# Moving the slot bookkeeping of an expert router forward, and reordering three VectorE steps of the expert loop

## The chip, the cores and the metric

The kernel runs on one core of a Trainium2 chip. The metric is the device time of one execution in microseconds (us), the median of three runs.

## What is computed

The input is 4096 tokens (16 sequences of 256) with 128 features, in float32. Four layers follow one another, each on the layer norm of `x` and added back to `x`: a gated linear attention, a mixture of experts, a small state-space layer, and a feed-forward layer on FP4-quantised values. The change lies in the mixture of experts alone:

```
scores = x_aD @ router_DE                         # 8 experts, the best one is taken
gates  = sigmoid(score of the best, else -inf)
mid    = silu((gate*x) @ w1[e]) * ((gate*x) @ w3[e])      # 128 -> 352
routed = mid @ w2[e]                              # 352 -> 128
shared = (silu(x @ ws1) * (x @ ws3)) @ ws2        # for every token
x      = x + shared + routed
```

## The kernel before, in words

Every engine has its own instruction stream, and the order in each is written out by hand; semaphores tie them together. There are three blocks with a barrier of all engines between them. `phase_ab` holds attention, and after it the shared expert and the routing. `phase_c` is the loop over the routed experts. `phase_d` does the last two layers.

**The tail of phase_ab.** The shared expert runs in eight groups of 512 tokens. On TensorE, `group(n)` is three `up(n, f)` (six 128x512 matmuls each) with two halves of `down(n-1)` between them. ScalarE applies Silu (`gated_up`), VectorE multiplies the two halves (`hidden`) and adds results to `x` (`add`). `up(n, f)` waits for the `hidden` of two steps before, `down(n, 0)` for the third `hidden` of its group. In the gaps stands the routing. VectorE's `one_hot` finds each token's expert; TensorE's `count_and_rank` counts; VectorE's `bases`, `positions` and `slot_parts` turn that into a slot number for each token; `slot_places` (four parts, L925) and `slot_rows` (L920) write one-hot factors; GpSimd multiplies two copies of the latter by gate and token number (L498, L501); TensorE's `slots` (64 matmuls, L1211) turn them into a table of which token stands in which slot; VectorE's `slot_table` copies the table out (L938); and GpSimd issues indirect DMAs (`gather`, L193, two for each pair of slot tiles, four pairs in this block) that fetch the token rows. In the same gaps ScalarE and GpSimd split the expert weights into high and low parts: `expert_high` (L657) and `expert_low` (L487, which waits for its `expert_high`). The last two gathers of the block stand behind the last `expert_low` on GpSimd.

**phase_c.** 5120 slots are 20 pairs of 128-row tiles. Iteration j of each engine is skewed. TensorE in iteration j: transposes of pair j+1 (L1494), the down product of pair j-2 (L1502), the first up product of pair j, transposes of the hidden values of pair j-1 (L1524), the second up product of pair j (L201 to L203). The transposes of pair k wait for semaphore `s_rg` to reach k+1. It is counted up by VectorE's scaling of the gathered rows of pair k by their gates (L1443), which stands in VectorE's iteration k-2, that is in iteration j-1 as seen from TensorE's iteration j. ScalarE does Silu (L1399) and copies of transposed values (L1406, L1415, L1416). VectorE in iteration j: low part of the transposed rows of pair j+1 (L1429), output copy of pair j-2 (L1436), row scaling of pair j+2 (L1443), hidden products of pair j (L1451, one for each tile), and in iterations 1 to 3 three steps each of FP4 preparation of the last layer's weights (`prepare`). GpSimd gathers pair k once the rows of pair k-4 have been scaled.

Of the kernel before, what the change touches and what calls it, by code (L numbers as in the profile page):

```python
# [205 lines left out]
def phase_ab(nc, io, g):  # L206
# [4 lines left out]
    with ExitStack() as ctx:  # L211
# [197 lines left out]
        def _(pool):  # L409
# [78 lines left out]
                                        w13p[:, 0, :, e, :].bitcast(F32), ALU.subtract).then_inc(s_wl, 1)  # L488

            by_slot = [P, T, SLOTS]  # L490
            for e_ in range(2):
                expert_low(e_)
            pool.wait_ge(s_gate, 1)
            nc.gpsimd.tensor_scalar(gate, gate, 0.5, 0.5, ALU.mult, ALU.add).then_inc(s_one, 1)
            expert_low(2)
            pool.wait_ge(s_pos, 5)
            pool.wait_ge(s_one, 4)
            nc.gpsimd.tensor_tensor(slot_high[:, :, SLOTS:], slot_high[:, :, 0:SLOTS],  # L498
                                    gate.unsqueeze(2).to_broadcast(by_slot), ALU.mult).then_inc(s_one, 1)
            pool.wait_ge(s_one, 5)  # L500
            nc.gpsimd.tensor_tensor(slot_high[:, :, 0:SLOTS], slot_high[:, :, 0:SLOTS],  # L501
                                    small[:, SLOTS + EXPERTS + P:].unsqueeze(2).to_broadcast(by_slot), ALU.mult).then_inc(s_part, 1)
            for e_ in range(3, 5):
                expert_low(e_)
            pool.wait_ge(s_tab, 2)
            for par in range(2):
                pool.wait_ge(s_xn2s[par], 8 * B)
            for k in range(2):
                gather(nc, g, k)
            for e_ in range(5, EXPERTS):  # L510
                expert_low(e_)
            for k in range(2, 4):
                gather(nc, g, k)
# [2 lines left out]
        def _(act):  # L516
# [161 lines left out]
            for n in range(2, GROUPS):  # L678
                for f in range(3):
                    gated_up(n, f)  # L680
                    if f == 0 and n + 1 < GROUPS:
                        token_high(n + 1)
                if n == 2:
                    act.wait_ge(s_hot, 1)
                    nc.scalar.activation(gate, best, ACT.Tanh, scale=0.5).then_inc(s_gate, 1)
                for e_ in ((0, 1), (2,), (3, 4), (), (5, 6), (7,))[n - 2]:
                    expert_high(e_)

        @blk_.vector
        def _(dve):  # L690
# [204 lines left out]
                nc.vector.tensor_tensor_scan(before.rearrange("p e t -> p (e t)"), padded[:, 0:ET],  # L895
                                             restart.rearrange("p e t -> p (e t)"), 0.0, ALU.add, ALU.mult).then_inc(s_hot, 1)

            def bases():
                dve.wait_ge(s_r, 1)
                step(nc.vector.tensor_scalar(over, ps_n, float(P - 1), None, ALU.add))  # L900
                step(nc.vector.tensor_scalar(count, over, 7, 7, ALU.arith_shift_right, ALU.logical_shift_left))
                step(nc.vector.tensor_tensor_scan(upto, ones[:, 0:EXPERTS], count, 0.0, ALU.mult, ALU.add))
                step(nc.vector.tensor_tensor(base, upto, count, ALU.subtract))

            def positions():
                step(nc.vector.tensor_tensor(rank, ps_r, base.unsqueeze(2).to_broadcast(spread), ALU.add))
                step(nc.vector.tensor_tensor(rank, rank, hot, ALU.mult))
                step(nc.vector.tensor_reduce(posf, rank.rearrange("p e t -> p t e"), AX.X, ALU.add))

            def slot_parts():  # L910
                nc.vector.tensor_copy(g["pos"][:, :], posf)
                step(nc.vector.tensor_copy(posi, posf))
                step(nc.vector.tensor_scalar(hii, posi, 7, 7, ALU.arith_shift_right, ALU.logical_shift_left))
                step(nc.vector.tensor_copy(hif, hii))
                step(nc.vector.tensor_tensor(low_pos, posf, hii, ALU.subtract))
# [44 lines left out]
            for n in range(2, GROUPS):  # L960
                for f in range(3):
                    hidden(n, f)
                    if f == 0 and n + 1 < GROUPS:
                        token_low(n + 1)
                    if (n, f) == (2, 2):
                        bases()
                    if (n, f) == (3, 0):
                        positions()
                    if (n, f) == (3, 1):
                        slot_parts()  # L970
                    if (3, 1) <= (n, f) <= (4, 1):
                        slot_places(3 * n + f - 10)
                    if (n, f) == (4, 2):
                        slot_rows()
                    if (n, f) == (6, 1):
                        slot_table()
                    if (n, f) == (6, 2):
                        slot_experts()
                add(n - 1)
            add(GROUPS - 1)  # L980

# [1 line left out]
        def _(pe):  # L983
# [207 lines left out]
            def group(n):  # L1191
                for f in range(3):
                    up(n, f)
                    if f < 2:
                        down(n - 1, f)
# [10 lines left out]
            def slots(part):  # L1206
                if part == 0:
                    pe.wait_ge(s_part, 1)
                pe.wait_ge(s_pos, part + 1)
                for t in range(8 * part, 8 * part + 8):  # L1210
                    last = nc.tensor.matmul(ps_s, slot_low[:, t, :], slot_high[:, t, :], start=(t == 0), stop=(t == T - 1))  # L1211
                if part == 3:
                    last.then_inc(s_tab, 1)
# [25 lines left out]
            up(2, 2)  # L1239
            group(3)  # L1240
            group(4)
            group(5)
            for part in range(4):
                slots(part)
            group(6)
            group(7)
            down(7, 0)
# [51 lines left out]
def phase_c(nc, io, g):  # L1299
# [3 lines left out]
    with ExitStack() as ctx:  # L1303
# [32 lines left out]
        def live(j):  # L1336
            return 0 <= j.off < PAIRS
# [85 lines left out]
        def _(dve):  # L1423
            def body(j):
                if live(j + 1):
                    k = j + 1
                    done(dve, s_xT, k)
                    done(dve, s_u, k, n=2, per=2, ago=2)
                    nc.vector.tensor_tensor(xT[:, k.par, 1, :, :], ps_t[:, 0:2, :], xT[:, k.par, 0, :, :].bitcast(F32),  # L1429
                                            ALU.subtract).then_inc(s_xL, 1)  # L1430
                if live(j + -2):
                    f = j + -2
                    done(dve, s_y, f)
                    if f.off >= 2:
                        dve.wait_ge(s_out[f.par], f.half(16))
                    nc.vector.tensor_copy(y[:, f.par, :, :], ps_y[:, 0:2, :]).then_inc(s_ys, 1)  # L1436
                if live(j + 2):
                    k = j + 2
                    dve.wait_ge(g["s_rows"][k.off % 4], 32 * (k.off // 4 + 1))
                    done(dve, s_xp, k, ago=2)  # L1440
                    for t in range(2):
                        c0 = 2 * k.off + t
                        last = nc.vector.tensor_scalar(rows[:, k.par, t, :], g["rows"][:, k.off % 4, t, :],  # L1443
                                                       g["slot_gate"][:, c0:c0 + 1], None, ALU.mult)
                    last.then_inc(s_rg, 1)
                if live(j):
                    for t in range(2):
                        done(dve, s_act, j, n=t + 1, per=2)
                        if t == 0:
                            done(dve, s_hp, j, n=2, per=2, ago=2)  # L1450
                        nc.vector.tensor_tensor(hid[:, j.par, t, :], act1[:, t, :], ps_3[:, t, 0:F], ALU.mult).then_inc(s_h, 1)  # L1451
                if 1 <= j.off < LO:
                    for n in range(3 * j.off - 3, 3 * j.off):
                        prepare(n)
# [527 lines left out]
```

## Time and profile before

| what | value |
|---|---|
| median of 3 runs | 643.13 us (643.05 to 643.78) |
| the profiled execution: its time / its span | 643.13 us / 641.4 us |
| TensorE matmul busy | 552.9 us (86%) |
| VectorE busy | 456.4 us (71%) |
| ScalarE busy | 306.6 us (48%) |
| GpSimd busy | 346.1 us (54%) |

The span is what the profiler saw between the first and the last instruction; the execution's own time is 1.7 us more. Times of rows count from the span's start. A shift of one block moves all that follows it, since the blocks are separated by barriers. PE is TensorE, DVE VectorE, ACT ScalarE, POOL GpSimd.

### The profile page before, as it was taken

How to read it: one execution, taken by the hardware profiler on the slowest of the kernel's cores; microseconds unless marked ns; L12 is line 12 of the kernel's file. 1: busy time of each engine (PE TensorE's matmuls, PEld its weight loads, DVE VectorE, ACT ScalarE, POOL GpSimd, SP SyncE). 2: the span in 40 equal slices, each digit the busy share in tenths (PEclk: the TensorE clock that was granted, in tenths of full speed). 3: DMA queues.
4: the chain of work that ended last, by engine and by line, in shares of the span. 5: the costliest groups of instructions: out<-in, count | busy, mean ns of one | idle time of the engine just before them, and what ended most of it. 6: DMA issues, size and time to landing. Idle time of an engine off the chain costs nothing. (4 is left out here: it accounts for less than half of the span.)

```text
span 641.4 us, 15224 instructions
## 1 busy us (share of the span) xinstructions
PE 552.9 (86%) x4532; PEld 450.0 (70%) x4533; DVE 456.4 (71%) x1215; ACT 306.6 (48%) x862; POOL 346.1 (54%) x519
## 2 busy tenths in 40 slices
PE   2799999999999997994879999287999999999965
PEld 1457667777776686874779998265787788788754
DVE  2679998999985569542874443127899999899873
ACT  1356667656675542230434444125455555645522
POOL 4468777777775302546654310555666657654221
PEclk9999999999999998997989999688999999999987
DMA  7001001001011432003222210110111110110000
GB/s 204 16 18 43 26 28 50 25 30 44 25 42 59 122 99 67 1 18 85 74 51 57 58 41 26 33 17 9 26 18 16 21 29 16 20 29 10 9 17 16
DMA packets 35320, 25.60 MB, mean 40 GB/s; under 512 B 4752, under 2 KB 31696, under 8 KB 35280
## 3 DMA queue, kind: packets, MB, share of 16 engines
q1 hardware_dynamic: 29392, 20.39, 10.7%
q0 software_dynamic: 5888, 4.72, 4.7%
q8 instruction: 20, 0.33, 0.2%
q14 instruction: 20, 0.16, 0.1%
HBM read 14.09 MB, written 6.82 MB: 33 GB/s over the span
## 5 line engine op out<-in xcount | busy, mean ns | idle before, releaser
L1107 PE MATMUL a_ps_a<-a_qx,a_kt 32*128 32x512 f32 x512 | 70.6, 641 | 1.0 <-DMA a_qx<-a_qs 1.0
L193 POOL DMA_INDIRECT rows<-xn_dram,slot_token x40 | 39.1, 977 | 46.3 <-DVE c_rows L1443 28.7
L1628 POOL DMA_INDIRECT x<-yg_dram,pos x32 | 55.4, 1732 | 11.8 <-issue 11.8
L1270 POOL TENSOR_TENSOR d_hq<-d_fh_v,d_fh_scale 128x352 f32<-128x352 f32 x32 | 27.9, 888 | 60.6 <-DVE d_fh_v L1296 60.6
L436 POOL TENSOR_SCALAR_AFFINE_SELECT a_at<-a_at 128x512 f32<-128x512 f32 x80 | 50.5, 650 | 16.4 <-ACT a_at L527 16.4
L527 ACT ACTIVATE a_at<-a_ps_a 128x512 f32<-128x512 f32 x80 | 44.5, 600 | 11.6 <-PE a_ps_a L1107 10.0
L1451 DVE TENSOR_TENSOR c_hid<-c_act,c_ps 128x352 f32<-128x352 f32 x40 | 20.5, 519 | 37.1 <-ACT c_act L1399 36.7
L1107 PEld LDWEIGHTS a_ps_a<-a_qx,a_kt 32*128 32x128 f32 x512 | 32.2, 192 | 17.7 <-issue 17.1
L1399 ACT ACTIVATE c_act<-c_ps 128x352 f32<-128x352 f32 x40 | 18.5, 463 | 48.4 <-PE c_ps L203 48.4
L201 PE MATMUL d_ps_A<-d_xnT,wmix 128*128 128x256 f32 x128 | 38.1, 298 | 1.6 <-DVE d_xnT L1807 0.9
L702 DVE TENSOR_TENSOR a_at<-a_ps_a,mask 128x512 f32<-128x512 f32 x48 | 32.8, 685 | 8.3 <-PE a_ps_a L1107 7.2
L202 PE MATMUL d_ps_A<-d_xnT,wmix 128*128 128x256 f32 x128 | 36.9, 288 | 0.0
L203 PE MATMUL d_ps_A<-d_xnT,wmix 128*128 128x256 f32 x128 | 36.8, 288 | 0.0
L878 DVE TENSOR_TENSOR a_hid<-a_act,a_ps_a 128x512 f32<-128x512 f32 (+1 forms) x24 | 16.4, 681 | 28.6 <-ACT a_act L653 28.5
L653 ACT ACTIVATE a_act<-a_ps_a 128x512 f32<-128x512 f32 (+1 forms) x24 | 14.2, 594 | 45.1 <-PE a_ps_a L203 45.1
L1031 PE MATMUL a_ps_o<-a_at,a_vpad 128*32 128x128 f32 x1024 | 34.6, 276 | 0.0
L1502 PE MATMUL c_ps_y<-w,c_hidT 128*128 (+1 forms) x240 | 32.0, 283 | 0.8 <-ACT c_hidT L1416 0.8
L462 POOL TENSOR_TENSOR a_kt<-a_e,a_rope 128x512 f32<-128x512 f32 x16 | 20.4, 1277 | 21.6 <-ACT a_e L563 21.6
L201 PE MATMUL c_ps<-w13p,c_xT 128*128 x80 | 30.8, 385 | 1.3 <-issue 0.3
L1502 PEld LDWEIGHTS c_ps_y<-w,c_hidT 128*128 128x128 f32 (+1 forms) x240 | 28.7, 193 | 2.3 <-issue 1.4
L1951 PEld LDWEIGHTS d_ps_G<-d_wd,d_hqT 128*128 128x128 f32 (+1 forms) x192 | 23.8, 199 | 8.6 <-issue 5.5
L787 DVE RECIPROCAL a_c<-a_c 128x128 f32<-128x128 f32 x32 | 29.2, 939 | 0.0
(287 smaller groups left out, 1794.1 us busy)
## 6 DMA issues: line engine op xcount, KB each, us to landing
a_qx<-a_qs SPq DMA_DIRECT2D x64, 64.0 KB, 1.9
a_at<-in_L_ffn_w_eDF_dram SPq DMA_DIRECT2D x16, 176.0 KB, 2.8
yg_dram<-c_y SPq DMA_DIRECT2D x20, 128.0 KB
xn_dram<-a_xn2s SPq DMA_DIRECT2D x16, 128.0 KB, 1.8
out_dram<-x SPq DMA_DIRECT2D x16, 128.0 KB, 1.8
w<-in_L_ffn_w_eFD_dram SPq DMA_DIRECT2D x2, 512.0 KB, 5.1
x<-in_L_attn_x_dram SPq DMA_DIRECT2D x1, 768.0 KB, 5.6
rows<-xn_dram,slot_token POOLq DMA_INDIRECT x40, 2.7
```

What stands on the lines that cost most here:

```text
L193: nc.gpsimd.indirect_dma_start(out=g["rows"][:, k % 4, t, :], out_offset=None, in_=g["xn2_dram"][:, :], in_offset=bass.IndirectOffsetOnAxi ...
L201: nc.tensor.matmul(to, left(0), right(0), start=start, stop=False)
L202: nc.tensor.matmul(to, left(0), right(1), start=False, stop=False)
L203: return nc.tensor.matmul(to, left(1), right(0), start=False, stop=stop)
L436: nc.gpsimd.affine_select(at[:, t, r, :, :], at[:, t, r, :, :], pattern=[[0, 4], [1, P]], compare_op=ALU.is_ge, fill=0.0, base=0, channel_ ...
L527: nc.scalar.activation(at[:, t, r, :, :], ps_a[:, r, :, :], ACT.Copy).then_inc(s_copied, 1)
L702: nc.vector.tensor_tensor(at[:, t, r, :, :], ps_a[:, r, :, :], mask[:, 0:1, :].to_broadcast([P, 4, P]), ALU.mult).then_inc(s_masked, 1)
L787: nc.vector.reciprocal(c[:, tile(t)], c[:, tile(t)]).then_inc(s_rc, 1)
L1031: last = nc.tensor.matmul(ps_o[32 * r:32 * r + 32, tile(t)], vpad[:, b.par, t, c0:c0 + 32], at[:, t, r, h, :], start=(t == 0 and h == 0), ...
L1107: last = nc.tensor.matmul(ps_a[:, r, :, :], kt[rows, b.par, c_, tile(t)], qx[rows, b.par, :, c_, tile(t)], start=(c_ == 0), stop=(c_ == 1))
L1502: last = nc.tensor.matmul(ps_y[:, t, :], hidT[0:fn, f.par, t, n, :], w2[0:fn, e_out[t], n, :], start=(n == 0), stop=(n == 2))
L1628: nc.gpsimd.indirect_dma_start(out=x[:, t, :], out_offset=None, in_=g["yg_dram"][:, :], in_offset=bass.IndirectOffsetOnAxis(ap=g["pos"][:, ...
```

## The change

1. VectorE merges `bases`, `positions` and `slot_parts` into one `positions()` after the third `hidden` of group 2; before they stood at (2,2), (3,0) and (3,1). `slot_rows` goes from (4,2) to (3,0), ahead of all `slot_places`; `slot_experts` from (6,2) to (4,2); `slot_table` from (6,1) to (5,1). As `slot_rows` is now the first to count `s_pos` up, the waits on it change by one.
2. TensorE runs the four `slots` parts ahead of `group(5)` and not behind it.
3. GpSimd runs one `expert_low` ahead of the slot products (before three), three behind them, then two gathers, the last four `expert_low`, two gathers. ScalarE's `expert_high` are distributed otherwise: the last two stand after group 6 and not one of them after group 7.
4. In phase_c's VectorE iteration, the hidden products of pair j now stand ahead of the row scaling of pair j+2.

```diff
@@ gpsimd
-            for e_ in range(2):
-                expert_low(e_)
             pool.wait_ge(s_gate, 1)
             nc.gpsimd.tensor_scalar(gate, gate, 0.5, 0.5, ALU.mult, ALU.add).then_inc(s_one, 1)
-            expert_low(2)
-            pool.wait_ge(s_pos, 5)
+            expert_low(0)
+            pool.wait_ge(s_pos, 1)
...
-            for e_ in range(3, 5):
+            for e_ in range(1, 4):
                 expert_low(e_)
...
-            for e_ in range(5, EXPERTS):
+            for e_ in range(4, EXPERTS):
                 expert_low(e_)
@@ scalar
-                for e_ in ((0, 1), (2,), (3, 4), (), (5, 6), (7,))[n - 2]:
+                for e_ in ((0,), (1,), (2, 3), (4, 5), (6, 7), ())[n - 2]:
@@ vector, shared expert
                     if (n, f) == (2, 2):
-                        bases()
+                        positions()
                     if (n, f) == (3, 0):
-                        positions()
-                    if (n, f) == (3, 1):
-                        slot_parts()
+                        slot_rows()
                     if (3, 1) <= (n, f) <= (4, 1):
                         slot_places(3 * n + f - 10)
                     if (n, f) == (4, 2):
-                        slot_rows()
+                        slot_experts()
-                    if (n, f) == (6, 1):
+                    if (n, f) == (5, 1):
                         slot_table()
-                    if (n, f) == (6, 2):
-                        slot_experts()
@@ tensor
-                pe.wait_ge(s_pos, part + 1)
+                pe.wait_ge(s_pos, part + 2)
...
-            group(5)
             for part in range(4):
                 slots(part)
+            group(5)
@@ phase_c, vector
                     nc.vector.tensor_copy(y[:, f.par, :, :], ps_y[:, 0:2, :]).then_inc(s_ys, 1)
+                if live(j):
+                    for t in range(2):
+                        done(dve, s_act, j, n=t + 1, per=2)
+                        if t == 0:
+                            done(dve, s_hp, j, n=2, per=2, ago=2)
+                        nc.vector.tensor_tensor(hid[:, j.par, t, :], act1[:, t, :], ps_3[:, t, 0:F], ALU.mult).then_inc(s_h, 1)
                 if live(j + 2):
                     k = j + 2
                     dve.wait_ge(g["s_rows"][k.off % 4], 32 * (k.off // 4 + 1))
...
                     last.then_inc(s_rg, 1)
-                if live(j):
-                    for t in range(2):
-                        done(dve, s_act, j, n=t + 1, per=2)
-                        if t == 0:
-                            done(dve, s_hp, j, n=2, per=2, ago=2)
-                        nc.vector.tensor_tensor(hid[:, j.par, t, :], act1[:, t, :], ps_3[:, t, 0:F], ALU.mult).then_inc(s_h, 1)
```

## Rows read from the trace of the kernel before

**Rows 1.** Stretches of phase_c: busy us (and instructions) by engine, clock, DMA, GB/s.
```profile
297.40:304.80 7.40, 5.04 (x16) 4.20 (x17) 2.78 (x9) 1.23 (x3) 5.71 (x8) 0.50 0.60 155
304.80:328.60 23.80, 17.34 (x117) 15.69 (x115) 21.34 (x32) 9.06 (x29) 15.35 (x11) 0.98 0.22 60
328.60:334.45 5.85, 5.81 (x33) 5.71 (x34) 2.60 (x7) 1.83 (x6) 3.79 (x4) 0.71 0.30 77
334.45:389.44 54.99, 54.10 (x385) 50.59 (x384) 26.61 (x72) 25.89 (x84) 15.09 (x16) 1.00 0.21 49
```
**Rows 2.** Timeline, one steady iteration: start, us, engine, line; idle before and releaser.
```profile
375.53 0.32 PE L203 MATMUL c_ps<-w13p,c_xT 128*128 x1
...
375.69 0.38 PE L1494 MATMUL c_ps_t<-mask,c_rows 128*128 128x128 f32 x2
375.88 0.46 ACT L1399 ACTIVATE c_act<-c_ps 128x352 f32<-128x352 f32 x1 [0.20 <-PE c_ps L203]
...
376.38 0.52 DVE L1451 TENSOR_TENSOR c_hid<-c_act,c_ps 128x352 f32<-128x352 f32 x1 [1.01 <-ACT c_act L1399]
376.82 0.42 DVE L1429 TENSOR_TENSOR c_xT<-c_ps_t,c_xT 128x256 fp32r<-128x256 f32 x1
...
380.29 0.38 PE L1494 MATMUL c_ps_t<-mask,c_rows 128*128 128x128 f32 x2
```
**Rows 3.** Timeline of TensorE, the transposes that waited for rows.
```profile
314.25 0.44 PE L1494 MATMUL c_ps_t<-mask,c_rows 128*128 128x128 f32 x2 [1.53 <-DVE c_rows L1443]
...
320.25 0.43 PE L1494 MATMUL c_ps_t<-mask,c_rows 128*128 128x128 f32 x2 [1.30 <-DVE c_rows L1443]
...
328.64 0.44 PE L1494 MATMUL c_ps_t<-mask,c_rows 128*128 128x128 f32 x2 [3.54 <-DVE c_rows L1443]
```
**Rows 4.** Timeline of VectorE at those waits.
```profile
313.72 0.47 DVE L1443 TENSOR_SCALAR c_rows<-rows,slot_gate 128x128 f32<-128x128 f32 x2
314.11 0.94 DVE L1451 TENSOR_TENSOR c_hid<-c_act,c_ps 128x352 f32<-128x352 f32 x2
...
323.61 3.92 DVE L1270 TENSOR_TENSOR wq<-c_w_v,c_w_scale 128x1120 f32<-128x1120 f32 x1
```
**Rows 5.** Timeline of all engines at the end of phase_ab.
```profile
291.71 0.69 DVE L882 TENSOR_TENSOR x<-x,a_ps_o 128x512 f32<-128x512 f32 x1 [2.44 <-PE a_ps_o L1186]
...
294.31 0.94 POOL L193 DMA_INDIRECT rows<-xn_dram,slot_token  x1 [0.30 <-issue]
297.42 0.52 POOL L1377 MEMSET c_wraw<- 128x512 f32 x1 [2.16 <-POOLq L211]
```
**Rows 6.** Timeline of TensorE in groups 3 to 6 of phase_ab.
```profile
243.74 0.47 PE L201 MATMUL a_ps_a<-a_tokens,ws 128*96 128x512 f32 x1 [0.54 <-DVE a_hid L878]
...
250.63 2.38 PE L1186 MATMUL a_ps_o<-ws,a_hid 128*128 128x128 f32 x12 [2.50 <-DVE a_hid L878]
...
265.93 7.37 PE L1211 MATMUL a_ps_t<-a_vpad,a_qx 128*128 128x80 f32 x64 [0.83 <-POOL a_vpad L501]
273.09 0.48 PE L201 MATMUL a_ps_a<-a_tokens,ws 128*128 128x512 f32 x1
```
**Rows 7.** Timeline of GpSimd in groups 4 to 7 of phase_ab.
```profile
260.78 2.34 POOL L498 TENSOR_TENSOR a_vpad<-a_vpad,a_kt 128x1280 f32<-128x1280 f32 x1 [12.32 <-DVE a_vpad L920]
263.20 2.67 POOL L501 TENSOR_TENSOR a_vpad<-a_vpad,small 128x1280 f32<-128x1280 f32 x1
...
279.23 1.24 POOL L193 DMA_INDIRECT rows<-xn_dram,slot_token  x1 [10.06 <-DVE slot_token L938]
```
**Rows 8.** Timeline of VectorE in groups 2 to 5 of phase_ab.
```profile
240.74 1.62 DVE L903 TENSOR_TENSOR a_qs<-a_qs 128x8 f32<-128x8 f32 x1
...
248.75 1.23 DVE L925 TENSOR_TENSOR a_qx<-a_kt,small 128x1024 f32<-128x1024 f32 x1
...
259.22 1.48 DVE L920 TENSOR_TENSOR a_vpad<-a_kt,small 128x1280 f32<-128x1280 f32 x1
...
261.82 1.85 DVE L870 TENSOR_TENSOR a_tokens<-xn2T,a_tokens 128x512 fp32r<-128x512 f32 x1
```

More of the change, by code:

```diff
@@ L896, in one_hot, with positions @@
                                              restart.rearrange("p e t -> p (e t)"), 0.0, ALU.add, ALU.mult).then_inc(s_hot, 1)
-            def bases():
+            def positions():
                 dve.wait_ge(s_r, 1)
@@ L903, in bases @@
                 step(nc.vector.tensor_tensor(base, upto, count, ALU.subtract))
-            def positions():
                 step(nc.vector.tensor_tensor(rank, ps_r, base.unsqueeze(2).to_broadcast(spread), ALU.add))
@@ L908, in positions @@
                 step(nc.vector.tensor_reduce(posf, rank.rearrange("p e t -> p t e"), AX.X, ALU.add))
-            def slot_parts():
                 nc.vector.tensor_copy(g["pos"][:, :], posf)
```

## The prediction

> **What bounds the kernel now.** I read three things in this order. First the page, for the shares: TensorE is 86% busy, so the question in each block is whether it waits, and for whom. Then the stretches of phase_c. From the eighth transposes (334.45) to the twentieth (389.44) TensorE is busy for 54.10 of 54.99 us at a granted clock of 1.00, while VectorE has 26.61 us of work [rows 1]. These are 12 iterations, so one takes 54.99 / 12 = 4.58 us, and 375.69 to 380.29 is one of them [rows 2]. Before that stretch TensorE is held up: the transposes of the fifth, sixth and seventh pair wait 1.53, 1.30 and 3.54 us for scaled rows [rows 3], because VectorE is full with weight preparation (21.34 of 23.80 us busy [rows 1]). Last the timelines of the end of phase_ab. TensorE and VectorE are done by 291.71 + 0.69 = 292.40, but GpSimd's last gather ends at 294.31 + 0.94 = 295.25, and the next block starts at 297.42 [rows 5]. So the end of phase_ab is set by GpSimd, phase_c by TensorE with a start that VectorE sets, and phase_d is not touched.
>
> **Part 4 of the change, the order in phase_c.** This is the large term. TensorE begins iteration j with the transposes of pair j+1, and these need the row scaling that stands in VectorE's iteration j-1. Before the change that scaling came ahead of the hidden products of pair j-1, and was done while the up products still ran. In the new order it comes behind them. The second hidden product of pair j-1 needs the second up product of pair j-1, and that is TensorE's last work before the very transposes in question. TensorE takes its work in order, so the chain closes: up product, Silu, hidden product, row scaling, transposes, with nothing of TensorE's beside it.
>
> The length comes from one steady iteration. The transposes start at 375.69, when the up product has been issued; its hidden product starts at 376.38, 0.69 us later, and VectorE's next instruction 0.44 us after that, at 376.82 [rows 2]. There the row scaling would now stand. From its start to the transposes that wait for it, 313.72 to 314.25, it is 0.53 us [rows 3, 4]. The wait is 0.69 + 0.44 + 0.53 = 1.66 us in each iteration, and the iteration 4.58 + 1.66 = 6.24 us.
>
> How many iterations? There are 20 pairs. The rows of the first two are scaled before any hidden product exists; the other 18 sit behind one. That is 18 x 1.66 = 29.9 us. Not all of it is new. The fifth to seventh transposes waited for the same semaphore already, 1.53 + 1.30 + 3.54 = 6.4 us together [rows 3]; VectorE can now prepare weights while TensorE works, because the chain leaves it more idle time, so I let the new wait replace the old ones. The iteration behind the 3.54 us wait ran at a granted clock of 0.71 and took 334.45 - 328.64 = 5.8 us instead of 4.58 [rows 1, 3]; without the long wait that 1.2 us goes. The part costs 29.9 - 6.4 - 1.2 = 22.3 us.
>
> What hides nothing: the hidden products move 0.39 us forward at most (313.72 to 314.11 [rows 4]), and only where VectorE, not Silu, is late, which is in the three iterations with preparation. In the steady stretch VectorE stands idle for 1.01 us ahead of the hidden product and waits for Silu [rows 2], so nothing is won there. The gathers are issued later, since each waits for a row scaling four pairs back, but they have four iterations to land.
>
> Bounds: the wait could be as short as 1.4 us (if the scaling's first tile overlaps more) and as long as 1.9 (a longer wake-up), so 25 to 34 us in all, less 7.6. The weight preparation adds an unknown. Its step L1270 took 3.92 us beside GpSimd work [rows 4]; if it meets that again behind the new, later rows, about 2 us of the 6.4 are not replaced. Bounds for the part: +18 to +26.
>
> **Parts 1 and 2, TensorE in the tail of phase_ab.** Merging the bookkeeping costs VectorE the same instructions, placed earlier. By following VectorE instruction by instruction, the first `hidden` of group 3 comes 1.0 us later: about 2.4 us of work moves ahead of it, and one step that took 1.62 us [rows 8] beside an `expert_low` falls back to some 0.2, because only one `expert_low` is left there. `slot_rows` (1.48 us [rows 8]) then goes ahead of the second `hidden`, which ends 0.9 us later than before. When `slot_rows` is done, GpSimd starts its two products of 2.34 and 2.67 us [rows 7], which before ran with little beside them. Now VectorE's first two `slot_places` (1.23 us each [rows 8]) want to run in the same time. The trace shows what happens then: the token step L870 took 1.85 us beside L498 [rows 7, 8] and ended just after it. So I let the first `slot_places` wait for L498, and the second for L501. The `hidden` that releases `down(3, 0)` ends at 250.9, where before the product started at 250.63 [rows 6]. The waits of TensorE, 0.54 and 2.50 us among them [rows 6], thus come back under other names, and I expect the end of group 4 within -1.5 to +0.2 us of before: the lower end if the clock stays up.
>
> The Trainium skill has a rule on this, in SBUF — State Buffer, section "SBUF: two separate sides": GpSimd and a VectorE instruction with two SBUF inputs take one pair of ports as an exclusive lock for a whole instruction. The trace agrees, with the 1.85 us just named. Without the lock the sum would be some 1.8 us lower.
>
> The `slots` then run right behind group 4. They took 7.2 us, 265.93 to 273.09, after a wait of 0.83 for GpSimd [rows 6]. In the new order GpSimd's products are done some 4 us before, so the 0.83 goes. TensorE's total work is the same; its end moves from 291.7 to between 289.2 and 290.9, I take 290.0, and VectorE's last add is done 0.7 us later, at 290.7.
>
> **Part 3, GpSimd at the end of phase_ab.** The slot table is now copied out after the second `hidden` of group 5, at about 269.5 to 271, where the first gather of before started at 279.23 [rows 7]. Four gathers, four `expert_low` of 1.7 us and four gathers follow, the last two `expert_low` held until group 6 is through. They end between 287 and 289, ahead of TensorE. So GpSimd no longer sets the end; VectorE at 290.7 does. The turn into the next block was 297.42 - 295.25 = 2.2 us [rows 5]. I keep it, though an engine that isn't last may leave less; it lies between 0 and 2.2. Phase_c starts at 290.7 + 2.2 = 292.9, that is 4.5 us sooner. Bounds: -7 (short turn, clock stays up) to -2 (TensorE as late as before, and a little more lock).
>
> **Sum.** The profiled execution took 643.13 us, equal to the median, with a span of 641.4. 643.1 - 4.5 + 22.3 = 660.9 us. Phase_d starts later and is otherwise the same.
>
> **The rivals.** (a) The clock falls in phase_c. Idle time of 1.66 us in each 6.24 could pull the granted clock down. The row for it: 1.53 and 1.30 us of waiting six us apart, with a clock of 0.98 over that stretch; against it, 0.71 after the 3.54 us wait [rows 1, 3]. The iteration at 0.71 took 1.2 us more; 1/0.71 - 1 is 0.41, so at 0.5 it would be 1.2 / 0.41 = 3 us more. If half of the 18 iterations ran so, 27 us come on top: 688 us. The Trainium skill warns of this in TensorE: Matmul & The Clock Gate, section "HAM oscillation — how this bites in real kernels": bursts with waits between them can start each burst at the low clock. The two short waits above speak against it here, so I give it little.
>
> (b) The transposes are not held after all, and only the front end counts. This is the faster side. It would be so if the rows that a transpose needs were scaled one VectorE iteration earlier than I read. Then part 4 costs nothing, or wins 0.39 us in each of three preparation iterations, about 1 us, and the time is 643.1 - 4.5 - 1 = 637.6. The count of rows speaks against it: the fifth transposes, at 314.25, wait for the scaling at 313.72, which directly precedes the hidden products at 314.11 [rows 3, 4].
>
> (c) The tail of phase_ab gains nothing: the lock, or the clock after the waits, makes TensorE late by what GpSimd saves. Then 643.1 + 22.3 = 665.4.
>
> **How the numbers follow.** The forecast has 0.86, (a) 0.06, (b) 0.03, (c) 0.05. A measurement tells about 0.2% of this kernel from no change. Only (b) is faster: 0.03; no mixture of the others lands on the old time, so 0.01 for the same, and 0.96 for slower. The range takes both bounds of both terms without the farthest corners, 643.1 - 7 + 19 = 655 to 643.1 - 2 + 26 = 667, which holds (c) and leaves (a) and (b) out.
>
> **What would show it.** In the changed kernel's waits, the transposes L1494 wait for DVE c_rows L1443 in 18 of 20 iterations, some 1.7 us each; they start 6.2 us apart; TensorE's busy share in that stretch falls from 98% to about 73% with the clock at 1.00. Phase_c starts near 293, and GpSimd's last gather of phase_ab ends before VectorE's last add. The prediction is wrong if the transposes still start 4.6 us apart, if the clock in phase_c is well under 1.00, or if phase_c starts no sooner than 297.

## The result, and the profile after

The changed kernel takes 660.49 us, median of 4 runs (659.28 to 662.65), beside 643.45 for the kernel before on the same chip (643.05 to 645.68): ratio 1.026, 95% interval 1.022 to 1.030. It is slower by 17.0 us. The forecast was 660.9. The profiled execution took 662.3 us, its span 660.6. In the experiments, five executions that ran slower (668.9 and 712.9 us of the kernel before, 660.2 of e9, 644.7 of e10, 1777.9 of e11) are left out of the ratios but not of the medians. Line numbers shift a little: in the changed kernel the transposes are L1484, the row scaling L1439, the hidden product L1432, Silu L1389.

First the page of the changed kernel: shares, and the group of the transposes. The last field is the idle time ahead of the group and its releaser.

```profile
span 660.6 us, 15223 instructions
...
PE 555.4 (84%) x4532; PEld 448.4 (68%) x4533; DVE 455.0 (69%) x1215; ACT 308.1 (47%) x862; POOL 351.6 (53%) x519
...
L1484 PE MATMUL c_ps_t<-mask,c_rows 128*128 128x128 f32 x40 | 8.7, 300 | 31.3 <-DVE c_rows L1439 31.3
```

TensorE has nearly the same busy time (555.4 us against 552.9) in a longer span. Ahead of the transposes it now idles 31.3 us, all of it for scaled rows. The timeline of one steady iteration shows why; it answers to [rows 2] and [rows 3].

```profile
341.98 0.33 PE L203 MATMUL c_ps<-w13p,c_xT 128*128 x1
342.35 0.46 ACT L1389 ACTIVATE c_act<-c_ps 128x352 f32<-128x352 f32 x1 [0.23 <-PE c_ps L203]
342.84 0.52 DVE L1432 TENSOR_TENSOR c_hid<-c_act,c_ps 128x352 f32<-128x352 f32 x1 [1.10 <-ACT c_act L1389]
343.28 0.48 DVE L1439 TENSOR_SCALAR c_rows<-rows,slot_gate 128x128 f32<-128x128 f32 x2
343.89 0.43 PE L1484 MATMUL c_ps_t<-mask,c_rows 128*128 128x128 f32 x2 [1.58 <-DVE c_rows L1439]
...
350.22 0.44 PE L1484 MATMUL c_ps_t<-mask,c_rows 128*128 128x128 f32 x2 [1.50 <-DVE c_rows L1439]
```

The up product ends at 342.31; Silu, hidden product, row scaling and transposes follow one behind the other, and TensorE has nothing beside them. The stretches of phase_c over twelve such iterations and of the rest of the kernel (columns as in [rows 1]):

```profile
331.20:407.00 75.80, 56.47 (x385) 49.87 (x385) 27.42 (x72) 26.55 (x84) 16.96 (x18) 1.00 0.16 36
460.00:660.60 200.60, 176.23 (x1176) 150.08 (x1174) 170.74 (x521) 102.02 (x283) 109.66 (x166) 0.96 0.10 18
```

The same 385 TensorE instructions took 54.99 us before [rows 1] and take 75.80 now: 6.32 us per iteration, TensorE busy 74% of it, at a granted clock of 1.00. So the end of phase_c moved by 20.8 us in these twelve iterations alone.

The end of phase_ab in the changed kernel, all engines, answers to [rows 5]:

```profile
288.08 0.94 POOL L193 DMA_INDIRECT rows<-xn_dram,slot_token  x1 [0.30 <-issue]
...
290.94 0.69 DVE L880 TENSOR_TENSOR x<-x,a_ps_o 128x512 f32<-128x512 f32 x1 [2.44 <-PE a_ps_o L1176]
291.92 0.53 POOL L1367 MEMSET c_wraw<- 128x512 f32 x1 [2.90 <-POOLq L211]
291.95 0.64 DVE L1439 TENSOR_SCALAR c_rows<-rows,slot_gate 128x128 f32<-128x128 f32 x2 [0.33 <-PEq L211]
```

GpSimd is through at 289.02, ahead of VectorE at 291.63, and VectorE's first step of phase_c starts at 291.95, against a block start of 297.42 before [rows 5].

### The profile page after: what moved, and what is told of

Its sections match the earlier page's. It is cut to its first block and busy times, and to the rows that moved or that the text cites. A ratio compares the mean times of both kernels' runs of the same rounds, so it can differ in the third digit from the quotient of the medians.

```text
span 660.6 us, 15223 instructions
## 1 busy us (share of the span) xinstructions
PE 555.4 (84%) x4532; PEld 448.4 (68%) x4533; DVE 455.0 (69%) x1215; ACT 308.1 (47%) x862; POOL 351.6 (53%) x519
## 3 DMA queue, kind: packets, MB, share of 16 engines
q0 software_dynamic: 5888, 4.72, 4.6%
## 5 line engine op out<-in xcount | busy, mean ns | idle before, releaser
L1618 POOL DMA_INDIRECT x<-yg_dram,pos x32 | 57.9, 1808 | 11.8 <-issue 11.8
L1432 DVE TENSOR_TENSOR c_hid<-c_act,c_ps 128x352 f32<-128x352 f32 x40 | 20.8, 521 | 46.2 <-ACT c_act L1389 46.2
L1097 PEld LDWEIGHTS a_ps_a<-a_qx,a_kt 32*128 32x128 f32 x512 | 32.0, 192 | 17.7 <-issue 17.1
L1389 ACT ACTIVATE c_act<-c_ps 128x352 f32<-128x352 f32 x40 | 18.6, 464 | 49.7 <-PE c_ps L203 49.7
L1484 PE MATMUL c_ps_t<-mask,c_rows 128*128 128x128 f32 x40 | 8.7, 300 | 31.3 <-DVE c_rows L1439 31.3
```

The lines of the kernel that those rows point to most:

```text
L1097: last = nc.tensor.matmul(ps_a[:, r, :, :], kt[rows, b.par, c_, tile(t)], qx[rows, b.par, :, c_, tile(t)], start=(c_ == 0), stop=(c_ == 1))
L1618: nc.gpsimd.indirect_dma_start(out=x[:, t, :], out_offset=None, in_=g["yg_dram"][:, :], in_offset=bass.IndirectOffsetOnAxis(ap=g["pos"][:, ...
```

## The experiments

For each kernel I read three times from its profile: the start of phase_c (the first row scaling), its length up to phase_d's first instruction on GpSimd, and the rest. Before they are 297.45, 108.2 and 235.8 us; changed 291.95, 131.3 and 237.3. Over all kernels the rest varies from 234.5 to 238.3 although nothing in it is edited. Medians are of interleaved runs, ratios to the kernel before with their 95% interval.

**The two halves of the change.** First the changed kernel with the old order in phase_c:

```
 # e1_front_only, against the changed kernel: in VectorE's body(j)
                     y copy
-                    hidden products of pair j
                     row scaling of pair j+2
+                    hidden products of pair j
                     prepare
```

> Parts 1 to 3 of the change, with phase_c's VectorE order as before (row scaling ahead of the hidden products). Theory (closed chain: only the order in phase_c costs time): phase_c starts near 292 as in the changed kernel, 5.5 us sooner than before, and its steady iterations take 4.58 us; 638 to 640 us. Rival (the earlier slot bookkeeping itself costs time later, by its waits or by gathers that come at another time): 645 us or more.

639.38 us, ratio 0.992 (0.989 to 0.995), as the theory has it. Phase_c starts at 291.83. Then the kernel before with the new order alone (the reverse edit, on the kernel before):

> Part 4 alone on the kernel before. Theory (closed chain): 18 waits of 1.5 to 1.6 us at the transposes, iterations of 6.3 us, phase_c 23 us longer, phase_ab as before: 666 us. Rival (the loss needs both the new phase_ab and the new order): under 660 us.

665.63 us, ratio 1.037 (1.032 to 1.043). Its TensorE in phase_c:

```profile
346.61 0.43 PE L1494 MATMUL c_ps_t<-mask,c_rows 128*128 128x128 f32 x2 [1.58 <-DVE c_rows L1449]
...
352.94 0.44 PE L1494 MATMUL c_ps_t<-mask,c_rows 128*128 128x128 f32 x2 [1.50 <-DVE c_rows L1449]
```

The same waits, 6.3 us apart, with phase_ab's code as before. By the medians the front end is worth −4.6 us and the order +21.7 (both against 643.94), together +17.1; the whole change measured +17.0. The two parts add up.

**How far back must the scaling be?** The chain needs the second hidden product. One that only follows the first should not close it:

```
 # e3_scaling_between, against the changed kernel
-                    hidden products t = 0, 1
-                    row scaling
+                    hidden product t = 0
+                    row scaling
+                    hidden product t = 1
```

> The changed kernel, but the row scaling of pair j+2 stands between the two hidden products of pair j, not behind both. Theory (the chain is closed by the second hidden product, which needs TensorE's last up product): the first hidden product starts 1.5 us before the second, so the rows are ready within 0.15 us of the moment when the transposes can start; iterations of 4.6 to 4.75 us; 638 to 642 us. Rival (any hidden product ahead of the scaling does it, as VectorE or the later gathers are what is short): half or more of the loss stays, 650 us or more.

641.44 us, ratio 0.997 (0.995 to 1.000), and in the steady stretch TensorE's transposes run without a wait, 4.73 us apart (four iterations from the first line to the last):

```profile
341.74 0.43 PE L1485 MATMUL c_ps_t<-mask,c_rows 128*128 128x128 f32 x2
...
360.68 0.44 PE L1485 MATMUL c_ps_t<-mask,c_rows 128*128 128x128 f32 x2
```

Moving the scaling ahead of one 0.5 us instruction is what takes away the wait of 1.6 us in each iteration. It isn't quite free: 4.73 us is 0.15 more than the 4.58 of the old order. The other way to open the chain is on TensorE: give it work to do ahead of the transposes.

```
 # e4_down_first, against the changed kernel: in TensorE's body(j)
-                transposes of pair j+1
                 down product of pair j-2
+                transposes of pair j+1
```

> The changed kernel with its VectorE order, but TensorE runs the down product of pair j-2 ahead of the transposes of pair j+1. Theory (the wait costs because nothing of TensorE's stands beside it): the down product takes 1.4 us and covers all but some 0.2 us of the 1.6 us; iterations of 4.6 to 4.9 us; 639 to 644 us. Rival (the later row scaling delays VectorE's or ScalarE's later steps, so that the loss stays wherever the transposes stand): 655 us or more.

A miss: 648.4 us, ratio 1.006 (1.003 to 1.009), iterations of 5.39 us and not 4.6 to 4.9. The scaling was now in time, but something else had lost its cover. In the timeline of that kernel:

```profile
353.94 0.47 DVE L1439 TENSOR_SCALAR c_rows<-rows,slot_gate 128x128 f32<-128x128 f32 x2
354.48 0.44 PE L1493 MATMUL c_ps_t<-mask,c_rows 128*128 128x128 f32 x2
355.46 0.43 PE L201 MATMUL c_ps<-w13p,c_xT 128*128 x1 [0.55 <-issue]
```

The idle 0.55 us ends in "issue": no semaphore held TensorE, its sequencer did. What stands there is the load of the two expert numbers into registers (L1471), 0.54 us each time:

```profile
L1471 PEldq TENSOR_LOAD <-slot_expert x20: 533/539/718, 289.6 to 396.5; - x20
```

In the kernel before this load runs at 376.7 under the down product, which starts at 375.92 and ends at 377.52. In e4 it runs at 354.6, right behind the late transposes, with nothing of TensorE's beside it. The test is to put it ahead of the wait:

```
 # e6_down_first_early_load, against e4_down_first
                 down product of pair j-2
+                load_experts(j); e_in = experts(j)
                 transposes of pair j+1
                 ...
-                load_experts(j); e_in = experts(j)
                 up products of pair j
```

> As the kernel with the down product first, and TensorE's load of the expert numbers (0.54 us) stands ahead of the wait for scaled rows, not behind it. In that kernel the iterations took 5.39 us and not the 4.6 to 4.9 expected, though the wait for rows was down to some 0.2 us. Theory (what stayed is the register load, which the late wait pushed out from under the down product): iterations of 4.8 to 4.9 us, 638 to 642 us. Rival (the rest is the wait for rows and the longer way through ScalarE and VectorE): 5.3 us again, 647 to 649 us.

636.41 us, ratio 0.991 (0.987 to 0.995), below what was expected. The iterations, three of them between these lines, are 4.72 us:

```profile
325.17 0.43 PE L1496 MATMUL c_ps_t<-mask,c_rows 128*128 128x128 f32 x2
...
339.34 0.41 PE L1496 MATMUL c_ps_t<-mask,c_rows 128*128 128x128 f32 x2
```

5.39 − 4.72 = 0.67 us per iteration for a load of 0.54. If it matters there, it may cost something in the old order too, though TensorE looked 98% busy there [rows 1]. The same move on e1:

> Parts 1 to 3 of the change with VectorE's order of before, and TensorE's load of the expert numbers at the start of its iteration. Theory (the 0.24 us that TensorE is idle ahead of the up product in each iteration is that load): iterations of 4.4 us instead of 4.58, 635 to 637 us. Rival (that gap is the issue of instructions, and the load is hidden already): the same as with parts 1 to 3 alone, 638 to 640 us.

635.32 us, ratio 0.988 (0.982 to 0.993). Two iterations between these lines are 4.26 us each, where the kernel before and e1 have 4.58. In those two, TensorE's matmuls are idle for only 0.08 us ahead of the up product, but its weight loads for 0.26; in e7 both are gone:

```profile
331.64 0.38 PE L1487 MATMUL c_ps_t<-mask,c_rows 128*128 128x128 f32 x2
...
340.16 0.38 PE L1487 MATMUL c_ps_t<-mask,c_rows 128*128 128x128 f32 x2
```

**Who sets the turn into phase_c?** The prediction kept a turn of 2.2 us that in the changed kernel is 0.3. If GpSimd's own end is what costs it, the kernel before must gain as well when its last four indirect DMAs are issued in phase_c instead:

```
 # e5_late_gathers, against the kernel before: GpSimd
 # end of phase_ab
-            for k in range(2, 4):
-                gather(nc, g, k)
 # phase_c, behind the two memsets
+            for k in range(2, 4):
+                gather(nc, g, k)
             for k in range(4, 8):
```

> The kernel before with one edit: the last four indirect DMAs of phase_ab are issued by GpSimd in phase_c, behind its two memsets and ahead of its other gathers. Theory (GpSimd's last gathers alone set the end of phase_ab): the block ends with VectorE's last add, phase_c starts some 4.5 us sooner relative to that end of TensorE's work; as the rows of pairs 2 and 3 land about 3 us later than before, up to 1 us is given back; 639 to 641 us. Rival (the turn between the blocks takes its 5 us after TensorE's last product whoever comes last): 643 to 645 us.

The turn went as expected, 0.3 us and not 5. The end of phase_ab in that kernel:

```profile
290.20 0.69 DVE L880 TENSOR_TENSOR x<-x,a_ps_o 128x512 f32<-128x512 f32 x1 [2.44 <-PE a_ps_o L1184]
...
291.18 0.52 POOL L1375 MEMSET c_wraw<- 128x512 f32 x1 [2.29 <-POOLq L211]
```

VectorE is through at 290.89, and the next block begins 0.3 us later. But the time did not fall: 644.89 us, ratio 1.003 (1.000 to 1.006), the number of the rival without its mechanism. Phase_c took 117.6 us instead of 108.2. Most of the loss lies in its first 20 us, on ScalarE:

```profile
304.30 0.46 ACT L1399 ACTIVATE c_act<-c_ps 128x352 f32<-128x352 f32 x1 [4.93 <-remote]
...
307.11 0.38 ACT L1415 ACTIVATE c_hidT<-c_ps_h 128x256 f32<-128x256 f32 x1 [2.35 <-remote]
309.92 2.93 PE L1502 MATMUL c_ps_y<-w,c_hidT 128*128 x12 [7.23 <-ACT c_hidT L1416]
```

ScalarE idled 4.93 us, its releaser is given as "remote" (no event of the core explains it), and TensorE waited 7.23 us for it. From the fourth transposes to the fifth it is 13.79 us, against 6.13 before. In e1 ScalarE idles 2.60 us ahead of the same Silu, TensorE's down product behind it 2.81, and phase_c is 112.1 instead of 108.2. It is in neither the kernel before nor the changed one. A second stretch adds to it in both: from the eighth transposes to the ninth e1 takes 8.11 us and e5 8.02, against 4.60 before. In e1 ScalarE is late there again (0.84 us, "remote", at 330.86), TensorE waits 1.77 us for it, and the granted clock from 329.5 to 337.6 is 0.79. As the iteration before it no longer has the slow clock of [rows 1] (4.68 us for 5.81), some 2.3 us of the loss lie in this stretch. So e1, with phase_c's start 5.6 us earlier, wins 4.6 us by the medians; e5, 6.2 us earlier (an estimated 1.5 of them not by the edit: its first GpSimd weight step at 237.47 is already 1.5 us ahead of the 238.98 before, see the last section), wins nothing.

**The weight preparation.** It keeps VectorE full in iterations 1 to 3 of phase_c, three steps in each [rows 1, 4]. One step in each of nine iterations instead:

```
 # e8_front_spread_prepare, against e1_front_only
-                if 1 <= j.off < LO:
-                    for n in range(3 * j.off - 3, 3 * j.off):
-                        prepare(n)
+                if 1 <= j.off < 10:
+                    prepare(j.off - 1)
```

> Parts 1 to 3 of the change with VectorE's order of before, and the nine steps of weight preparation spread over nine iterations of phase_c, one each, and not three in each of three. Theory (the waits for scaled rows that the kernel before has, 6.4 us and a slow iteration behind them, are VectorE's three steps in a row): nearly all of them go, 632 to 635 us. Rival (the steps cost the same wherever they stand, since they collide with GpSimd's weight work): 637 us or more.

632.73 us, ratio 0.984 (0.978 to 0.990), as expected; phase_c 104.2 us, with ScalarE's delay of 4.80 us still in it. Both edits together:

> Parts 1 to 3 of the change, VectorE's order of before, the early load of the expert numbers and the nine preparation steps spread over nine iterations. If the two gains add (about 4 us from the load, 6 us from the spreading, against parts 1 to 3 alone): 628 to 630 us. If the load only fills time that the waits for preparation left: 632 us, as with the spreading alone.

626.58 us, ratio 0.973 (0.963 to 0.983), the best of all: 16 us under the kernel before (642.56 beside it). Its four runs are few and far apart, 622.5, 623.8, 629.4 and 660.2, so the size is rough. TensorE is busy for all of this stretch, and its transposes are 4.25 us apart:

```profile
310.00:380.00 70.00, 70.00 (x529) 68.04 (x528) 41.96 (x100) 35.88 (x117) 24.83 (x23) 1.00 0.22 53
```

Its profiled execution is flattered by about 3.8 us, for its phase_c starts at 288.2 (last section); phase_c itself takes 98.5 us, 9.7 less than before.

**ScalarE's delay.** The first one comes while phase_c's weights are loaded, so one theory was that these transfers cause it. e10 holds the loads; e11 is its control. Both start the nine steps in iteration 4:

```
 # e11_front_spread_from_4, against e8_front_spread_prepare
-                if 1 <= j.off < 10:
-                    prepare(j.off - 1)
+                if 4 <= j.off < 13:
+                    prepare(j.off - 4)
 # e10_front_spread_held_loads, against e11: SyncE, ahead of phase_c's 13 weight loads
             sp.wait_ge(s_zero, 2)
+            sp.wait_ge(s_act, 4)
```

> The control of the held loads: the same kernel with the preparation in iterations 4 to 12, and the loads issued at the start of phase_c as before. Both theories: the delay of ScalarE's third Silu is there, 632 to 633 us.

> Parts 1 to 3, VectorE's order of before, the preparation one step each in iterations 4 to 12, and phase_c's 13 weight loads held until ScalarE has done four Silu. In three kernels whose phase_c starts early, ScalarE's third Silu comes 3 to 5 us after its input was ready, in the stretch in which these loads keep the DMA engines full. Theory (the loads cause this delay of ScalarE): with the loads held, the third Silu follows its matmul within 0.4 us, and the time is 3 to 4 us under the kernel with the same preparation and no hold: 628 to 630 us. Rival (the delay belongs to the start of the block, some 10 us after it, whatever the DMA engines do): the delay stays, 632 us.

The control took 632.23 us (631.5, 631.8, 632.7 and 1777.9), ratio 0.983 (0.978 to 0.988), as e8. With the loads held it was 637.85, ratio 0.994 (0.990 to 0.999): worse than the control and than both forecasts, a miss. Its timeline shows one thing gained and two lost. ScalarE's early delay is 0.92 us only, and from the fourth transposes to the fifth it is 5.58 us (8.66 in the control). But the stores of y stand in the same queue behind the loads, so VectorE's copy of y waits 2.82 us for one. GpSimd's product for the weights waited too, and now runs beside VectorE's next row scaling, which takes 2.94 us where most take 0.47. The seventh transposes wait 3.14 us for it:

```profile
300.97 0.46 ACT L1390 ACTIVATE c_act<-c_ps 128x352 f32<-128x352 f32 x1 [0.92 <-remote]
...
313.07 0.40 POOL L1373 COPY c_wtap<-c_win 128x256 f32<-128x256 f32 x1 [13.03 <-DMA wc<-in_L_attn_w_C_dram]
313.29 0.42 DVE L1427 COPY c_y<-c_ps_y 128x256 f32<-128x256 f32 x1 [2.82 <-DMA yg_dram<-c_y]
313.44 2.86 POOL L1374 TENSOR_TENSOR c_wtap<-c_win,c_cw 128x1024 f32<-128x1024 f32 x1
313.63 2.94 DVE L1434 TENSOR_SCALAR c_rows<-rows,slot_gate 128x128 f32<-128x128 f32 x2
```

The larger loss comes later, at the tenth transposes. ScalarE, VectorE and TensorE all stand, for nothing that the trace names:

```profile
334.04 0.42 DVE L1427 COPY c_y<-c_ps_y 128x256 f32<-128x256 f32 x1 [4.99 <-remote]
334.11 0.46 ACT L1390 ACTIVATE c_act<-c_ps 128x352 f32<-128x352 f32 x1 [6.13 <-remote]
334.98 0.68 PE L1484 MATMUL c_ps_t<-mask,c_rows 128*128 128x128 f32 x2 [3.17 <-DVE c_rows L1434]
```

The two iterations around it take 7.93 and 7.20 us, where the control needs 4.65 and 4.55. Of the 7.3 us by which phase_c is longer than in the control (111.0 for 103.7), 5.9 are these. The last weight load had been issued at 309, and the DMA engines are 15% busy from 331 to 335.

Last, the hold with the early register load as well:

> Everything together: parts 1 to 3, VectorE's order of before, the early load of the expert numbers, preparation in iterations 4 to 12 and the weight loads held. If the loads cause ScalarE's delay: 625 to 627 us. If not: as without the hold, 628 to 630 us.

635.54 us, ratio 0.987 (0.979 to 0.995), a miss again. Here ScalarE is late early on in spite of the held loads (the line below), and again later: 5.14 us at 335.38, with TensorE's down product waiting 5.73 behind it and 12.11 us from one transposes to the next:

```profile
302.24 0.38 ACT L1406 ACTIVATE c_hidT<-c_ps_h 128x256 f32<-128x256 f32 x1 [1.69 <-remote]
```

So the weight loads are not what delays ScalarE, or not alone: the largest delay of all came when none was under way. The cause stays open. Each of these kernels has one trace, so how often the delays come is not known either.

## Why the prediction was right

The two terms of the sum were −4.5 and +22.3. In the profiled executions they are −5.5 (291.95 − 297.45) and +23.1, and the unedited rest is 1.5 us longer; together 19.1 us, and the spans differ by 19.2. The medians differ by 17.0. That the forecast of 660.9 lies 0.4 us from the median is therefore partly luck: two errors of about 1 us cancel, and single executions differ by more than that.

**The order in phase_c: right, +22.3 predicted, +23.1 measured** (131.3 − 108.2). The chain is the one described, link for link: in the iteration shown, 0.86 us from the start of the last up product to its hidden product, 0.44 to the scaling, 0.61 to the transposes (0.85, 0.44 and 0.53 by [rows 2 to 4]). All 20 transposes wait, the first two for the block's beginning. The 31.3 us of the page hold 1.74 and 1.32 for those two, which leaves 28.2 / 18 = 1.57 us for each of the others. This is not the predicted 1.66 measured: the prediction counted from where the transposes would have been issued, 0.16 us after the start of the last up product, and the profile counts idle time from that matmul's end, 0.33 us after its start. The 0.17 us between is the overlap that the transposes had with the matmul ahead of them and lost. Counted as predicted, the wait is 0.70 + 0.44 + 0.61 = 1.75 us in the iteration shown and 1.66 in the next, where the last link is 0.53. The iteration is 6.32 us where 6.24 was predicted, and that last link is most of the difference. The register load of e4 has no part in it. In the changed kernel it runs at 345.0, under the down product as before, and the idle time of the weight loads ahead of the up products over the twelve iterations (us in total, times, longest) is the same in the kernel before and in the changed one:

```profile
PEld c_ps L201 <- issue: 3.1, 12, 0.3
```

The old waits went as assumed. From the first to the eighth transposes the changed kernel needs 331.19 − 292.64 = 38.55 us, against 36.31 before, only 2.24 more for the seven iterations; the wait of 3.54 us [rows 3] is 2.08 in the changed kernel. The assumption that VectorE could meet GpSimd again behind the later rows was not needed: the preparation step that took 3.92 us [rows 4] takes 1.32 in the changed kernel.

```profile
306.74 0.20 DVE L1278 TENSOR_SCALAR c_w_scale<-c_w_amax 128x70 f32<-128x70 f32 x1
...
313.55 0.74 DVE L1271 TENSOR_SCALAR c_w_k<-c_w_k 128x1120 f32<-128x1120 f32 x1
...
320.32 1.32 DVE L1260 TENSOR_TENSOR wq<-c_w_v,c_w_scale 128x1120 f32<-128x1120 f32 x1
```

**TensorE in the tail of phase_ab: right in kind, 0.9 us off.** Its last product ends at 290.90 (290.94 by VectorE's wait for it), predicted 290.0, at the upper end of the bounds 289.2 to 290.9. The changed kernel's TensorE there, answering to [rows 6]:

```profile
244.89 0.48 PE L201 MATMUL a_ps_a<-a_tokens,ws 128*96 128x512 f32 x1 [1.60 <-DVE a_hid L876]
...
250.99 2.36 PE L1176 MATMUL a_ps_o<-ws,a_hid 128*128 128x128 f32 x12 [1.84 <-DVE a_hid L876]
...
258.15 7.27 PE L1201 MATMUL a_ps_t<-a_vpad,a_qx 128*128 128x80 f32 x64
```

The waits came back under other names, 1.60 and 1.84 for 0.54 and 2.50; the hidden product that ends the second was forecast for 250.9 and ended at 250.94; the wait of 0.83 ahead of the slots is gone. `slot_places` was held by GpSimd, as read from the token step. First GpSimd in the changed kernel, then VectorE:

```profile
246.92 2.34 POOL L496 TENSOR_TENSOR a_vpad<-a_vpad,a_kt 128x1280 f32<-128x1280 f32 x1 [6.15 <-DVE a_vpad L914]
249.34 3.20 POOL L499 TENSOR_TENSOR a_vpad<-a_vpad,small 128x1280 f32<-128x1280 f32 x1
```

```profile
247.35 2.99 DVE L919 TENSOR_TENSOR a_qx<-a_kt,small 128x1024 f32<-128x1024 f32 x1
...
250.86 2.76 DVE L919 TENSOR_TENSOR a_qx<-a_kt,small 128x1024 f32<-128x1024 f32 x1
```

2.99 and 2.76 us for a step that takes 1.23 alone [rows 8]. Each ends 1.08 us after GpSimd's instruction does, so each seems to wait that one out and then run, and the second of GpSimd's waits in its turn (3.20 against 2.67 before [rows 7]). The trace agrees with the rule of the Trainium skill that the prediction cites (SBUF — State Buffer, section "SBUF: two separate sides").

The prediction put its lower end on a clock that stays up. It did not stay up: the granted clock was 0.55 from 251.3 to 255.0, as in the kernel before. e9 has the same code up to phase_c, and there it was 1.00 in these 3.7 us. The changed kernel first, then e9:

```profile
251.30:255.00 3.70, 3.70 (x17) 3.31 (x16) 3.70 (x4) 0.00 (x0) 3.70 (x2) 0.55 0.00 0
```

```profile
251.30:255.00 3.70, 3.70 (x27) 3.23 (x25) 3.70 (x6) 0.95 (x2) 1.78 (x1) 1.00 0.23 61
```

**GpSimd at the end of phase_ab: the end right, the turn wrong.** GpSimd's last gather ends at 289.02 (predicted 287 to 289) and no longer sets the end of the block. The step that failed is the one that kept the turn at 2.2 us. From GpSimd's last step of phase_ab to its next one there are 2.2 us [rows 5] to 2.9, in the changed kernel and in e5 too; but when VectorE ends last, phase_c's first VectorE step starts 0.3 us behind it, in the changed kernel, e1 and e5 alike. Together: TensorE 0.9 later, turn 1.9 shorter, phase_c at 291.95 instead of 292.9. That these two errors point opposite ways and leave only 1.0 us is luck too.

**The rivals.** (a), a falling clock: out, 1.00 over the twelve iterations with a wait in each. But its argument, that short waits leave the clock alone, is weaker than it looked: in phase_ab of the changed kernel TensorE waited 1.60, 0.94 and 1.84 us between 243 and 251, and the clock fell; in e9 the waits there are 1.58, 0.98 and 1.85, and it did not. (b), transposes not held: out, by e1 and e3, which give the time back as soon as the scaling stands ahead of the second hidden product. (c), no gain in phase_ab: out by phase_c's start, and by e1's 4.6 us. But e5 shows a way to it that the prediction did not have: an earlier start of phase_c can be lost again by ScalarE's delays. The changed kernel did not show that delay; its rest was 1.5 us longer than before, which is within what the unedited rest varies by.

## What to carry to other kernels

Before moving a producer's step, find the instruction of the consumer that it now lands behind: if that instruction itself waits for the consumer's last work, the chain closes, and the consumer idles for its whole length in each iteration, 1.74 us here; one instruction further up costs 0.15 (e3). Register loads of an in-order engine belong ahead of its waits, in a loop that looks 98% busy too: 0.3 us of 4.58 in each iteration, some 3 to 4 us in all (e7 beside e1). Where preparation for a later block rides in a loop, one step per iteration is cheaper than three in a few (e8), and a gain at the end of one block counts only once the next block has been seen to keep it (e5).

## What the runs showed of the hardware

**TensorE's clock rises late at the start of the kernel, and not always at the same moment.** Matmuls of one line and shape in the kernel before, ahead of the rise and behind it (min, median and max in ns, then first and last start in us):

```profile
L203 PE MATMUL a_ps_c<-a_xnT,a_wallp x4: 415/415/416, 14.8 to 24.5; 128*128 128x256 f32 x4
```

```profile
L203 PE MATMUL a_ps_c<-a_xnT,a_wallp x4: 279/283/285, 38.7 to 49.8; 128*128 128x256 f32 x4
```

Their weight loads take 330 ns and 189; in e1 from 333.5 to 336.5, where the granted clock is 0.50, the lower of the two levels, such a weight load takes 0.33 us, and behind that stretch 0.19. So TensorE runs at the lower level for its first stretch. In the kernel before the trace's record of the clock begins at 36.2 us, in e2 at 25.5, and in e2 that is where these durations change (0.41 us at 25.09, 0.28 at 25.50). The 1.00 that the profile prints for 27 to 31 us comes from no record. The sixteen score products in that stretch are slow in the kernel before and fast in e2:

```profile
L1107 PE MATMUL a_ps_a<-a_qx,a_kt x16: 1056/1056/1215, 27.1 to 29.8; 32*128 32x512 f32 x16
```

```profile
L1107 PE MATMUL a_ps_a<-a_qx,a_kt x16: 587/587/692, 27.1 to 28.5; 32*128 32x512 f32 x16
```

The record begins at 36 to 37 us in the kernel before, the changed one, e1, e3, e7, e8 and e12, at 30 to 31.5 in e5, e6, e9, e10 and e11, and at 25.5 and 26.0 in e2 and e4. With that and the fall near 250 us, which e4, e9, e10 and e11 do not have, the starts of phase_c fall into line. With the new front end it starts at 291.8 to 292.0 (late rise), 290.1 (e6, earlier rise), 288.2 to 288.5 (e9, e10 and e11, earlier rise and no fall) and 287.2 (e4, earliest rise and no fall); with the old one at 297.45, and at 293.8 in e2. No edit lies ahead of the rise, so it varies by itself; why is open. It may be a part of why executions of one kernel differ by up to 1% (639.3 to 646.0 for the kernel before beside e1).

**ScalarE can be held for up to 6 us by nothing that the trace names.** About 10 us into phase_c it idles 2.60 us in e1, 4.93 in e5, 5.31 in e7 and 4.80 in e8; TensorE's down product behind it waits 2.81 in e1, 7.23 in e5, and also 3.08 in e9 and 2.32 in e11. Some 45 us into it ScalarE idles 6.13 us in e10 and 5.14 in e12, long after the weight loads.

**A register load on TensorE's sequencer takes 0.54 us.** In e4 it shows as 0.55 us of "issue" ahead of the next matmul; in the old order it shows as 0.26 us of idle time of the weight loads, and putting it ahead of the wait won 0.3 us per iteration (e7).
